# Attention of a graph network with expert layer: stationary operands of 128 columns instead of 125

## The reference, cut to what matters

```python
q = jnp.einsum('btd,hds->bhts', h, Wq)
k = jnp.einsum('btd,hds->bhts', h, Wk)
v = jnp.einsum('btd,hds->bhts', h, Wv)
scores = jnp.einsum('bhts,bhus->bhtu', q, k) * d ** (-0.5)
scores = jnp.where(causal, scores, -jnp.inf)
att = jax.nn.softmax(scores, axis=-1)
out = jnp.einsum('bhtu,bhus->bhts', att, v)
x = x + out @ Wp + bp
```

## Time and profile before

| what | value |
|---|---|
| median of 3 runs | 1222.88 us (1220.94 to 1224.35) |
| the profiled execution's own time | 1224.95 us |
| its span, first to last instruction | 1222.9 us |
| granted TensorE clock, mean over the span | 0.942 of full speed |
| TensorE matmuls, busy | 1074.7 us, 6178 matmuls |
| attention, first score to the last scaled pv | 531.60 to 626.61 us of the span |

### The profile page before, as it was taken

One profiled execution on the slowest core, in us unless ns is written; L12 is line 12 of the kernel. 1 busy time (PEld: TensorE's weight loads), 2 busy tenths in 40 slices (PEclk: granted clock), 3 DMA queues, 4 the chain that ended last, 5 costly groups with the idle time before them and its releaser, 6 DMA issues.

```text
span 1222.9 us, 19243 instructions
## 1 busy us (share of the span) xinstructions
PE 1074.7 (88%) x6178; PEld 685.5 (56%) x6179; DVE 762.0 (62%) x1289; ACT 557.4 (46%) x740; POOL 339.4 (28%) x183
## 2 busy tenths in 40 slices
PE   5989688999699679999989408999999999999997
PEld 3555477546557446568877303545555555555554
DVE  7676678774536755358867418983112989889811
ACT  2676556303221134257642018683113777778511
POOL 3100000380003512034001327462000566566400
PEclk9999889999889879989999558999999999999999
DMA  8920200022401440020000289997001999999501
GB/s 295 370 72 1 103 1 1 1 103 76 78 1 64 78 78 1 1 100 2 2 2 1 62 194 378 340 372 262 13 26 32 352 376 375 364 386 363 214 16 28
DMA packets 98378, 170.63 MB, mean 140 GB/s; under 512 B 38611, under 2 KB 38691, under 8 KB 98330
## 3 DMA queue, kind: packets, MB, share of 16 engines
q1 hardware_dynamic: 88138, 145.33, 34.3%
q0 software_dynamic: 6016, 16.80, 4.5%
q10 hardware_dynamic: 4176, 7.87, 2.0%
HBM read 153.19 MB, written 18.79 MB: 141 GB/s over the span
## 4 chain that ended last, share of the span: by engine, by line
PE 66%; DVE 14%; issue 9%; POOL 4%; DMA 3%; ACT 2%; DVEq 1%; POOLq 0%; ACTq 0%; SPq 0%
PE psum L1329 32%; PE psum L1519 12%; PE psum L1540 12%; PE psum L1318 4%; DVE area L1270 3%; POOL area L635 2%; PE psum L1366 2%; DVE smalls L920 2%; DMA sorted_tokens<-area,smalls 1%; PE psum L1528 1%; DMA low<-in_L_ffn_W_dram 1%; DVE low L932 1%; DVE low L1036 1%; DVE low L1037 1%; PE psum L1381 1%
## 5 line engine op out<-in xcount | busy, mean ns | idle before, releaser
L1329 PE MATMUL psum<-area,low 128*125 128x256 f16 (+2 forms) x1080 | 250.4, 393 | 21.1 <-DVE low L1115 11.0
L1270 DVE TENSOR_TENSOR area<-low,area 128x1536 f16<-128x1536 f32 x96 | 231.9, 2456 | 18.9 <-ACT area L849 18.7
L635 POOL TENSOR_TENSOR area<-low,area 128x1536 f16<-128x1536 f32 x48 | 184.3, 3839 | 162.4 <-ACT area L849 162.3
L849 ACT ACTIVATE area<-low 128x1536 f16<-128x1536 f32 x144 | 209.5, 1482 | 36.0 <-DMA low<-in_L_ffn_W_dram 31.2
L1519 PE MATMUL psum<-area,low 128*128 128x512 f16 x972 | 221.4, 382 | 0.0
L1540 PE MATMUL psum<-area,low 128*128 128x384 f16 x1296 | 218.0, 326 | 2.3 <-DVE area L1270 1.1
L1329 PEld LDWEIGHTS psum<-area,low 128*125 128x125 f16 (+1 forms) x1080 | 151.2, 151 | 115.3 <-issue 64.0
L1329 PE MATMUL psum<-area 125*125 125x64 f16 (+9 forms) x1076 | 163.1, 304 | 12.2 <-DVE area L1256 8.0
L1540 PEld LDWEIGHTS psum<-area,low 128*128 128x128 f16 x1296 | 126.1, 98 | 82.7 <-issue 3.0
L1519 PEld LDWEIGHTS psum<-area,low 128*128 128x128 f16 x972 | 95.7, 98 | 114.1 <-issue 3.9
L1329 PEld LDWEIGHTS psum<-area 125*125 125x125 f16 (+2 forms) x1076 | 118.4, 160 | 42.0 <-issue 14.4
(11 more groups left out here) (202 smaller groups left out, 1239.7 us busy)
## 6 DMA issues: line engine op xcount, KB each, us to landing
low<-in_L_ffn_W_dram SPq DMA_DIRECT2D x144, 768.0 KB, 7.0
area<-in_L_gnn_W_dram SPq DMA_DIRECT2D x2, 3072.0 KB, 12.1
area<-in_L_gnn_Wr_dram SPq DMA_DIRECT2D x2, 3072.0 KB, 16.5
sorted_tokens<-area POOLq DMA_DIRECT2D x3, 1792.0 KB, 16.6
sorted_totals<-area POOLq DMA_DIRECT2D x3, 1792.0 KB, 28.8
low<-sorted_tokens ACTq DMA_DIRECT2D x11, 384.0 KB, 3.2
low<-sorted_totals ACTq DMA_DIRECT2D x9, 384.0 KB, 4.2
area<-in_L_ffn_Wv_dram SPq DMA_DIRECT2D x6, 384.0 KB, 6.3
```

What stands on the lines that cost most here:

```text
L635: pool.tensor_tensor(low_, raw_view(u), high_, ALU.subtract).then_inc(pool_low_ok, 1)
L849: act.activation(unit_parts(u)[0], raw_view(u), ACT.Copy).then_inc(high_ok, 1)
L1270: dve.tensor_tensor(low_, raw_view(u), high_, ALU.subtract).then_inc(dve_low_ok, 1)
L1329: ins = pe.matmul(place(name)[0:parts, at:at + w], left(q), right(q)[:, at:at + w], start=(q == 0), stop=(q == k - 1))
```

## The change

The places for the queries get 128 columns for each block instead of 126, of which the last three stay zero. The products of scores and of pv then take 128 columns of stationary operand, and write 128 rows of PSUM of which the readers still use 125. The transposes take 128 columns of `abuf`, the last of each item excepted, which still takes 125; the three further columns are the first of the next block, and the rows that come of them are not read. `attT` also has room for 128 columns; GpSimd clears it once with a new memset, whose signal ScalarE and VectorE await before the attention loop.

```diff
-        QW, KW = T * PP // 2, FC * NP // 2
+        QW, KW = T * 64, FC * NP // 2
...
+            done(pool, ("QT", FC - 1))
+            pool.memset(A(4, 0, 2 * T * 128, P), 0.0).then_inc(zeroed, 1)
...
             n = T * FH
+            act.wait_ge(zeroed, 2)
...
-            act.wait_ge(zeroed, 2)
+            act.wait_ge(zeroed, 3)
...
             dve.wait_ge(consts, 2)
+            dve.wait_ge(zeroed, 2)
...
+            def turn_scores(name, k, tile):
+
+                free(pe, name)
+                for q in range(k):
+                    w = 128 if q < k - 1 else P
+                    ins = pe.transpose(place(name)[0:w, q * 128:q * 128 + P], tile[:, q * P:q * P + w], ident[0:P, 0:P])
+                ins.then_inc(made, 1)
+
...
-                    product(("score", i), 3, lambda k: QT[h][PARTS[k][0]][:, t, 0:P],
-                            lambda k: KT[PARTS[k][1]][:, h // 2, :], (t + 1) * P, P)
+                    product(("score", i), 3, lambda k: QT[h][PARTS[k][0]][:, t, :],
+                            lambda k: KT[PARTS[k][1]][:, h // 2, :], (t + 1) * P, 128)
...
-                    turn(("attT", i - 2), t + 1, abuf[(i - 2) % ROWS][:, 0:(t + 1) * P])
+                    turn_scores(("attT", i - 2), t + 1, abuf[(i - 2) % ROWS])
...
-                    product(("pv", i - 3), 3 * (t + 1), lambda k: attT[(i - 3) % 2][PARTS[k % 3][0]][:, k // 3, 0:P],
-                            lambda k: Vt[PARTS[k % 3][1]][:, k // 3, h * HS:(h + 1) * HS], HS, P)
+                    product(("pv", i - 3), 3 * (t + 1), lambda k: attT[(i - 3) % 2][PARTS[k % 3][0]][:, k // 3, :],
+                            lambda k: Vt[PARTS[k % 3][1]][:, k // 3, h * HS:(h + 1) * HS], HS, 128)
```

## The result

The changed kernel takes 1212.32 us (median of 6 runs, 1207.48 to 1214.65), the kernel before 1223.21 us (6 runs, 1220.94 to 1225.04): ratio 0.9909, 95% interval 0.989 to 0.9929, 10.9 us less. The forecast was 1212.1 us, 10.8 us less.

The account below looks back on a forecast made before the run. Prediction: TensorE alone sets the pace at k = 4 and 5. 12 x (0.39 + 0.20 + 0.12 + 0.04 + 0.08) = 10.0 us, minus 0.2, plus 1.0 in the tail: 10.8 us off, median 1212.1 us, 0.8 range 1206.5 to 1218.5.

Parts of the forecast that it names:

- What a fast load ahead of 64 columns costs: pv products: 35 ns each instead of 57, between bounds of 30 and 50; saves 0.33 us a pass at k = 5.
- The rival of a 50 ns floor: pv: load and product never follow in under 50 ns, so a product saves 7 ns; 1217.4 us, chance 0.13.
- the rival of an issue rate of 57 ns: pv gains nothing as 57 ns is the issue rate; only 113-column pieces and transposes gain, 1221.6 us; chance 0.10.
- Scores and transposes: At k = 5, three score pieces of 113 columns give 0.02 us a pass, transposes at 10 ns each 0.04 us.
- The passes: Attention, twelve passes per item size: 0.39, 0.20, 0.12, 0.04 and 0.08 us off a pass for k = 5 to 1.
- the tail: End of attention: three pv of 15 products lie bare on the chain behind L1175, saving 3 x 0.33 = 1.0 us.
- guess for the meshing: Engines that close don't mesh without gaps: 0.20 us a pass taken of VectorE's 0.24 at k = 4, 0.12 of 0.18 at k = 3.
- the ring: Waits from subtraction through pv, next score, next transposes and copy back to subtraction, two passes long; the prediction spoke of a "way round".
- What takes over: At k = 5 a pass would need 1.90 us of TensorE and 1.78 of VectorE, so nearly the whole 0.39 is kept.
- way round: Transposes, L809, L1175, pv: limits k = 2 to 0.04 of 0.13 us a pass, k = 1 to 0.08.
- The slower rival: The half clock lasts through k = 2 and 3, ending at 1227.8 us; chance 0.05, with all else that could cost time.
- its cover: GpSimd's new memset of about 1.2 us hides behind 29 us of key products before its waiters, costing nothing.

Follow-up runs that it names:

- the run without pv: The changed kernel with pv back at 125 columns and rows, scores and transposes kept at 128: 1218.35 us, ratio 0.9978 to the kernel before.
- The runs with the copy on ScalarE: One unread ScalarE copy of 128 fp32 columns added per pass, in both kernels: before with it 1229.48 us (ratio 1.0051), changed with it 1218.87 us (0.996).

## Why the prediction was right

*What a fast load ahead of 64 columns costs* was the term no row of before could give: bounded by 30 and 50 ns, taken as 35. It is 28 ns, just under the lower end. The step from a load that lasts 41 ns less to a pv bound by its columns held, and so did the reading that missing rows do no harm. The rival of a 50 ns floor and the rival of an issue rate of 57 ns both fall with that row; the kernel with 127 columns rules the second out as well, since it issues the same instructions and keeps the old time.

*Scores and transposes* were put at 0.06 us a pass with k = 5 and gave 0.09, as the run without pv showed. The transposes gave 0.60 - 0.55 = 0.05 us where 0.04 were forecast, so 10 ns of the 47 by which their load gets shorter was about right. The rest, 1.69 - 1.65 = 0.04 us, came with the scores, where 0.02 were forecast.

*The passes.* By the windows the change gave 0.70, 0.50, 1.47 and 2.24 us for k = 1 to 4, where 1.0, 0.5, 1.4 and 2.4 were forecast; k = 5 and the tail gave 3.72 + 1.46 = 5.2 us for a forecast of 4.7 - 0.2 + 1.0 = 5.5. The sum came out at 10.1 for 10.8. That the medians lie 10.9 us apart makes the forecast no better than that: their interval is 8.7 to 13.5 us.

At k = 3 and 4 the amounts were right for another reason than the one given. The prediction had TensorE alone set the pace at k = 4 and 5, and took the gains at k = 3 and 4 from VectorE's idle time, less a guess for the meshing. The runs with the copy on ScalarE show that the ring was level with the pace at both. A ring over two passes gives back half of what pv saves: 9 x 29 / 2 = 0.13 us at k = 3 and 12 x 29 / 2 = 0.17 us at k = 4. With only pv changed the windows gave (16.97 - 15.64) / 12 = 0.11 and (21.14 - 19.11) / 12 = 0.17 us. For TensorE alone as the pace, k = 5 remains.

*What takes over* is where the reasoning was weaker than the number. The prediction made TensorE's 1.90 us the pace at k = 5, with VectorE's 1.78 close below. TensorE needs less, since pv is cheaper: in its timeline after, the starts of one pass lie 600.55 - 598.77 = 1.78 us apart.

```profile
598.77 1.40 PE L1333 MATMUL psum<-area 125*128 125x64 f16 x21
600.00 0.71 PE L1449 MATMUL psum<-smalls,low 125*128 125x125 f32 x5
600.55 1.40 PE L1333 MATMUL psum<-area 125*128 125x64 f16 x21
```

VectorE needs 1.69 (20.72 / 11 less the copy's 0.19). Measured were 1.90, and the ring sets them. The prediction named this "way round" for k = 1 and 2 only, and reckoned it as gaps in the meshing elsewhere. That pv costs 7 ns less than assumed and that a third limit stood at 1.90 cancelled. So the 1.90 us were met by luck, and the time fitted for a reason that was in part another. A pv in the tail holds 0.61 us of the chain, too, where some 0.5 were expected, though the tail as a whole gave more than forecast (1.46 us for 1.0).

*The slower rival.* At the low clock (0.5, 1.2 GHz) stood 10.24 us after as before: the stretch from 533.89 to 544.13 us has 0.51 of full clock, and the window with k = 3 is at 1.00. It didn't outlast k = 1 but for the first 2 us of k = 2. The stretch before:

```profile
534.40:544.64 10.24, 10.24 (x69) 9.26 (x68) 7.36 (x49) 6.64 (x29) 6.03 (x1) 0.50 0.51 189
```

*Small things.* The memset stayed under its cover. The prediction's upper end of its own forecast, 1214.5 us, does not come out of its terms: half of 12 x (0.20 + 0.12) is 1.9 us, which gives 1214.0. Nothing else hangs on it.

## What to carry to other kernels

Look at how long weight loads last, apart from the products: a stationary operand of 128 columns, padded with zeros or with whatever lies next to it, may load faster than one of 125 or 127 (98 ns against 139 and 140 here). It pays where the moving operand streams for less time than separates two such loads: here with 64 columns (30 ns against 57), while with 250 to 500 columns, at k = 2 to 4, scores and transposes together gave under 0.02 us a pass. When the full engine gets faster, work out the ring of waits through all engines and divide it by the passes it spans before you name the next limit, because here, with k = 5, it stood above the busy time of each engine. A small extra operation put into one engine's stream helps to tell what the limit is. A step on the ring over two passes showed by half (0.108 of 0.21 us), and work in spare time showed nothing (0.19 us on VectorE with k = 5). That work on a full engine would show whole is what one expects, but no run here has that case. And an engine whose rows have no gap need not be the limit.

## What the runs showed of the hardware

Of the widths in these runs only 128 columns have the short load: 139 ns at 125, 140 at 127, 98 at 128 in fp16, with 112, 125 and 128 rows alike at 128 columns. The Trainium skill (TensorE: Matmul & The Clock Gate, section on weight-path perf modes) says the same for fp16. It excludes FP32; here the fp32 loads of transposes go from 189 to 141 ns too (191 at 127 columns), and the five transposes of a pass take 0.55 us of the chain instead of 0.60.

A VectorE copy of 256 fp32 columns from SBUF to SBUF took 0.27 us alone, and up to 5.92 us while GpSimd ran its long operation on Wp. By the timeline of the changed kernel with the extra copy, the first row is the copy, the second GpSimd's operation:

```profile
537.14 5.92 DVE L1185 COPY area<-area 125x256 f32<-125x256 f32 x1
...
536.81 6.10 POOL L563 TENSOR_SCALAR area<-area 128x2304 f32<-128x2304 f32 x1 [36.48 <-DMA area<-in_L_ffn_Wp_dram]
```

The copy's record ends at 543.06 us, 0.15 us behind GpSimd's operation (542.91). The next two copies, of 1.59 and 4.04 us, also end 0.15 us behind GpSimd's next two operations, at 545.23 and 549.86 us. Not every VectorE operation meets this: in the kernel before, the same GpSimd operation began at 538.61 us, and the twelve subtractions L1175 with k = 1, which read PSUM, kept 291 ns on average, one of them at 539.73 us 0.29. What it is in the copy that collides, these runs don't show.
